# One row tile of the adjacency loaded in 32 by 32 blocks and turned by VectorE

## The chip, the core and the metric

The kernel runs on one core of one Trainium2 chip. The metric is the device time of one launch in microseconds (us), the median of three runs. Within the program the times below count from the first instruction of the profiled execution.

## What is computed

Four graph layers in a row, each followed by a layer norm, on 1354 nodes with 256 features and one dense 1354 by 1354 float32 adjacency matrix `adj`. Only the first layer is touched here:

```python
# layer 1: binarised features and weight, aggregated over the adjacency
bw = sign(weight)
ba = maximum(sign(x), 0)
xw = ba @ bw.T
x  = layernorm(x + relu(adj @ xw))
# layers 2 to 4 then use adj as well: adj @ x, masked attention, mean over neighbours, softmax(...) * adj
```

## The kernel before

The nodes are cut into eleven tiles of 128 (the last has 74). Everything after the first layer reads the adjacency transposed, as `adjT` (128 partitions, 11 column tiles, 1408 wide), so the first layer builds `adjT` while it aggregates. Here is the work for row tile i:

- SyncE's queue (SP) loads the tile into one of three slots of `adj_rows` (L312). From the fourth tile on it first waits until the tile that used the slot has been turned.
- TensorE (PE) turns the tile with eleven transposes of 128 by 128 into three PSUM banks (`adj_turn`, L1302).
- ScalarE (ACT) copies each bank twice (`adj_evac`): into `adjT` (L494) and, rounded, into `hi` (L495).
- VectorE (DVE) computes `lo`, the rest `adjT - hi`, for the first two bank groups (`lower_bits`, L755). GpSimd (POOL) does it for the third (L375).
- TensorE aggregates: `agg_a(i)`, L1375, is 22 matmuls, for each of eleven k one with `hi` and one with `lo`. Before k = 0 it waits for the first `lo` group, before k = 4 for the second, before k = 8 for POOL's.
- VectorE finishes the tile (`finish_a`: L798, the statistics L782 to L785, whose last writes `veps`), POOL takes the reciprocal square root (`rstd`, L386), VectorE writes `nmr` (`shift_a`, L806), and ScalarE applies both (L527).

The order on each engine is written by hand. TensorE does `agg_a(i)` and then `adj_turn(i + 2)`, and before `agg_a(4)` a short `spread_dots` (L1358). VectorE's step i is: finish tile i, a few dot products (L814, from step 4 on; three of them in step 4), first `lo` group of tile i+2, `nmr` of tile i, second `lo` group of tile i+2. POOL's step i is `rstd` of tile i and then its `lo` group of tile i+2. ScalarE's is `adj_evac(i)` and then the norm of tile i-2. Every engine takes its instructions in order. When the eleventh `agg_a` is through, TensorE goes on with the second layer (`z_part`, L1394), which needs the normed features one tile at a time.

Of the kernel before, what the change touches and what calls it, by code (L numbers as in the profile page):

```python
# [9 lines left out]
ACT = mybir.ActivationFunctionType  # L10
AX = mybir.AxisListType

P = 128
# [29 lines left out]
def gnn_stack(nc, x, adj, w0, w_sa, a_sa, w_gcn, b_gcn, wa, ba, wb, bb, w2, b2, w3, out):  # L43
    N, D = x.shape
    T = -(-N // P)
    FULL = N // P
    TAIL = N - FULL * P
    NP = T * P
# [5 lines left out]
    BANKS_T = -(-T // EB)  # L54
# [16 lines left out]
    BLOCK = 32  # L71
    QUADS = P // BLOCK
    SUMB = [2, 5, 2]
    BLOCKED = NC + 1
    NB3 = [2, 3, 5]
    FIN4 = {1: 0, 5: 1, 8: 2}
# [8 lines left out]
    def grp(g):  # L85

        return g * EB, min(g * EB + EB, T)

    ctx = ExitStack()
    with ctx:  # L90
# [5 lines left out]
        def sem(name):  # L96
            return Count(ctx.enter_context(nc.semaphore(name)))
# [71 lines left out]
        def at(name, offset, shape, dt=F32):  # L169
            return nc.alloc_sbuf_tensor_at(name, shape, dt, offset=base + offset)  # L170

        adj_rows = at("adj_rows", 0, [P, 3, NP])
        hi = at("hi", 3 * LONG, [P, PARTS, T, P], F32R)
        lo = at("lo", 6 * LONG, [P, PARTS, T, P], F32R)
        xw = at("xw", 9 * LONG, [P, T, D], F32R)
# [42 lines left out]

        adj_in = [sem("adj_in_0"), sem("adj_in_1"), sem("adj_in_2")]
        adj_in_tail = sem("adj_in_tail")  # L220
        rows2_in = [sem("rows2_in_even"), sem("rows2_in_odd")]
        x_in = [sem(f"x_in_{n}") for n in range(PAIRS)]
        w0_in, w_in, wsa_in, a_in, col_in = sem("w0_in"), sem("w_in"), sem("wsa_in"), sem("a_in"), sem("col_in")
# [74 lines left out]
        def tiles(g):  # L298

            c0, c1, _ = chunk(g)  # L300
            return range(c0 // P, -(-c1 // P))

        def across(columns, n, r):

            return columns[0:r, n:n + 1].to_broadcast([r, P])

        @block.sync
        def _(sp):
            def load_rows(i):
                if i >= 3:  # L310
                    sp.wait_ge(adjT_turned.sem, (i - 2) * BANKS_T)
                sp.dma_start(adj_rows[:, i % 3, 0:N], adj[i * P:(i + 1) * P, :]).then_inc(adj_in[i % 3].sem, 16)  # L312

            sp.dma_start(w0n[:, :, :], w0.rearrange("(k p) d -> p k d", p=P)).then_inc(w0_in.sem, 16)
# [3 lines left out]
            sp.wait_ge(pads_zero.sem, 1)  # L318
            sp.dma_start(x_all[0:64, FULL, :], x[FULL * P:FULL * P + 64, :]).then_inc(x_in[PAIRS - 1].sem, 16)
            sp.dma_start(x_all[64:TAIL, FULL, :], x[FULL * P + 64:N, :]).then_inc(x_in[PAIRS - 1].sem, 16)  # L320
            for i in range(FULL):
                load_rows(i)
            sp.wait_ge(adjT_turned.sem, (FULL - 2) * BANKS_T)
            b = FULL % 3
            sp.dma_start(adj_rows[0:64, b, 0:N], adj[FULL * P:FULL * P + 64, :]).then_inc(adj_in_tail.sem, 16)
            sp.dma_start(adj_rows[64:TAIL, b, 0:N], adj[FULL * P + 64:N, :]).then_inc(adj_in_tail.sem, 16)
# [150 lines left out]
        def _(act):  # L477
# [8 lines left out]
            def adj_evac(i, groups=range(BANKS_T)):  # L486
                r = kk(i)
                if i >= PARTS:
                    act.wait_ge(agga_done.sem, i - PARTS + 1)
                for g in groups:  # L490
                    k0, k1 = grp(g)
                    act.wait_ge(adjT_turned.sem, i * BANKS_T + g + 1)
                    src = bank((i % 2) * BANKS_T + g, 0, (k1 - k0) * P).rearrange("p (k n) -> p k n", n=P)[:, :, 0:r]
                    nc.scalar.activation(adjT[:, k0:k1, i * P:i * P + r], src, ACT.Copy)  # L494
                    nc.scalar.activation(hi[:, i % PARTS, k0:k1, 0:r], src, ACT.Copy).then_inc(adjT_banks_read.sem, 1)  # L495
# [242 lines left out]
        def _(dve):  # L738
            own = Own(dve, dve_own.sem)

            nc.vector.memset(dots[:, 0, 0:P], 0.0).then_inc(zeros_ready.sem, 1)
            own.link(nc.vector.memset(x_all[:, FULL, :], 0.0))
            nc.vector.memset(adj_rows[:, :, N:NP], 0.0).then_inc(pads_zero.sem, 1)
            nc.vector.memset(rdeg[:, :], 0.0)
            nc.vector.memset(dent[:, :], 1.0)
# [4 lines left out]
            def lower_bits(i, groups=range(BANKS_T)):  # L750
                r = kk(i)
                for g in groups:
                    k0, k1 = grp(g)
                    dve.wait_ge(adjT_banks_read.sem, BANKS_T * i + g + 1)
                    last = nc.vector.tensor_tensor(lo[:, i % PARTS, k0:k1, 0:r], adjT[:, k0:k1, i * P:i * P + r],  # L755
                                                   hi[:, i % PARTS, k0:k1, 0:r], ALU.subtract)
                    last.then_inc(lo_ready.sem, 1)

            def positive(n):
                t0, t1 = 2 * n, min(2 * n + 2, T)  # L760
# [71 lines left out]
            for i in range(T):  # L832
                if i == 2:
                    dot_columns()
                finish_a(i)
                if i == 4:
                    dve.wait_ge(ubc_ready.sem, 1)
                    left_dot(0)
                    left_dot(1)
                if i >= 4:  # L840
                    left_dot(i - 2)
                if i + 2 < T:
                    lower_bits(i + 2, range(0, 1))
                shift_a(i)
                if i + 2 < T:
                    lower_bits(i + 2, range(1, LOW))
            left_dot(T - 2)
# [422 lines left out]
        def _(pe):  # L1270
# [12 lines left out]
            def adj_turn(i):  # L1283
                r = kk(i)
                if i == FULL:
                    pe.wait_ge(adj_in_tail.sem, 32)
                else:
                    pe.wait_ge(adj_in[i % 3].sem, 16 * (i // 3 + 1))
                for g in range(BANKS_T):
                    k0, k1 = grp(g)  # L1290
                    if i == 0:
# [87 lines left out]
            for i in range(T):  # L1379
                if i == 4:  # L1380
                    spread_dots()
                agg_a(i)
                if i + 2 < T:
                    adj_turn(i + 2)


# [420 lines left out]
```

## Time and profile before

| | us |
|---|---|
| median of three runs | 473.91 (473.73 to 473.94) |
| the profiled execution, its own time | 474.03 |
| its span, first to last instruction | 472.2 |
| first layer: first `agg_a` to the last | 13.2 to 53.3 |

The span is the part of the profiled execution that the trace covers; 1.8 us lie around it. Each row of a time line gives the start, the duration, the engine, the source line, the operation, output and input with their shapes, and in brackets the idle time before it with what ended it. Successive starts on one engine can be closer than the durations, since an engine overlaps the end of one instruction with the next.

### The profile page before, as it was taken

The page shows a single profiled execution, that of the slowest core. Times are in us where ns is not written, and L with a number is a line of the kernel's source. Part 1 is how long each engine was busy: PE and PEld are TensorE (multiplying, and loading weights), DVE is VectorE, ACT ScalarE, POOL GpSimd, SP SyncE. Part 2 cuts the span into 40 slices and gives each one's busy share as a digit, 9 for nine tenths or more (in the row PEclk, how much of TensorE's full clock was granted, in tenths as well). Part 3 has the DMA queues.
Part 4 walks back from the last instruction along what each step waited for, and adds up shares of the span by engine and source line. Part 5 has one row for each costly group of instructions (what it writes and reads, how often), then busy time and mean ns, then how long its engine had stood idle before and what let it go on. Part 6 is the DMA issues. An engine that isn't in the chain of part 4 may idle for free.

```text
span 472.2 us, 5614 instructions
## 1 busy us (share of the span) xinstructions
PE 461.6 (98%) x1838; PEld 302.9 (64%) x1838; DVE 373.1 (79%) x830; ACT 231.3 (49%) x408; POOL 189.2 (40%) x186
## 2 busy tenths in 40 slices
PE   8999999999999999999999999999999999999993
PEld 7999755545555588787544444554557546778882
DVE  4688799999998689858137746999955697899984
ACT  6979529991888543333434532442333475342200
POOL 1444665631425036954001541452440073456641
PEclk9999999999999999999999999999999999999999
DMA  8856310001359100000000000000000000000001
GB/s 304 279 177 184 128 36 0 1 1 59 117 185 202 32 0 1 0 1 1 0 1 0 0 1 1 1 0 0 1 1 1 0 1 1 0 20 16 22 24 40
DMA packets 16500, 21.73 MB, mean 46 GB/s; under 512 B 9328, under 2 KB 13060, under 8 KB 16472
## 3 DMA queue, kind: packets, MB, share of 16 engines
q1 hardware_dynamic: 14648, 19.28, 13.2%
q10 hardware_dynamic: 1360, 1.31, 0.8%
q0 software_dynamic: 464, 0.79, 0.7%
q8 instruction: 15, 0.25, 0.2%
q14 instruction: 13, 0.11, 0.1%
HBM read 19.99 MB, written 1.39 MB: 45 GB/s over the span
## 4 chain that ended last, share of the span: by engine, by line
PE 75%; DVE 18%; issue 4%; DMA 1%; POOL 1%; ACT 0%; SPq 0%; POOLq 0%; DVEq 0%
PE psum L1590 16%; PE psum L1433 11%; PE psum L1394 11%; PE psum L1690 8%; PE psum L1375 6%; PE psum L1627 6%; PE psum L1570 3%; DVE ST L1082 3%; PE psum L1302 3%; PE psum L1542 2%; PE psum L1456 2%; PE psum L1661 2%; DVE rm L1031 2%; PE psum L1484 2%; DVE stats L782 1%
## 5 line engine op out<-in xcount | busy, mean ns | idle before, releaser
L1590 PE MATMUL psum<-QT,xT 128*128 128x512 f32 (+3 forms) x264 | 108.0, 542 | 0.0
L459 POOL TENSOR_TENSOR es<-es,ST 128x512 f32<-128x512 f32 (+3 forms) x60 | 75.9, 1265 | 55.2 <-ACT ST L658 53.5
L653 ACT ACTIVATE ST<-psum 128x512 f32<-128x512 f32 (+3 forms) x66 | 36.1, 546 | 91.6 <-DVE rm L1031 81.8
L1590 PEld LDWEIGHTS psum<-QT,xT 128*128 128x128 f32 (+1 forms) x264 | 48.2, 186 | 42.5 <-issue 35.9
L1031 DVE TENSOR_TENSOR rm<-psum,rm 128x512 f32<-128x512 f32 (+3 forms) x60 | 37.4, 623 | 40.6 <-PE psum L1590 40.4
L1690 PE MATMUL psum<-Wh,ST 128*128 128x256 f32 (+3 forms) x242 | 55.1, 380 | 0.0
L1627 PE MATMUL psum<-ST,Wh 128*128 128x512 f32 (+3 forms) x132 | 54.4, 543 | 0.6 <-DVE ST L1082 0.6
L386 POOL TENSOR_TENSOR rstd<-veps,nhalf 128x1 f32<-128x1 f32 (+1 forms) x44 | 29.2, 664 | 64.0 <-DVE veps L785 64.0
L414 POOL TENSOR_TENSOR esumb<-esumb,eb 128x1354 f32<-128x1354 f32 (+1 forms) x10 | 34.5, 3450 | 46.3 <-ACT eb L560 46.3
L1433 PE MATMUL psum<-eb,x_all 128*128 128x512 f32 (+3 forms) x132 | 51.9, 542 | 0.0
L1394 PE MATMUL psum<-adjT,x_all 128*128 128x512 f32 (+3 forms) x132 | 50.1, 542 | 0.0
L658 ACT ACTIVATE ST<-ST 128x512 f32<-128x512 f32 (+3 forms) x66 | 37.8, 578 | 25.0 <-DVE ST L1078 22.4
L1690 PEld LDWEIGHTS psum<-Wh,ST 128*128 128x128 f32 (+3 forms) x242 | 44.5, 186 | 8.2
L1082 DVE TENSOR_TENSOR ST<-ST,adjT 128x512 f32<-128x512 f32 (+3 forms) x66 | 46.8, 709 | 1.5 <-POOL es L459 1.5
L1627 PEld LDWEIGHTS psum<-ST,Wh 128*128 128x128 f32 (+1 forms) x132 | 24.9, 190 | 25.5 <-issue 19.2
L1394 PEld LDWEIGHTS psum<-adjT,x_all 128*128 128x128 f32 (+1 forms) x132 | 25.0, 190 | 24.7 <-issue 21.1
L1078 DVE TENSOR_TENSOR ST<-ST,psum 128x512 f32<-128x512 f32 (+3 forms) x66 | 40.0, 614 | 0.1
L1433 PEld LDWEIGHTS psum<-eb,x_all 128*128 128x128 f32 (+1 forms) x132 | 24.8, 190 | 22.6 <-issue 19.6
L456 POOL COPY es<-ST 128x512 f32<-128x512 f32 (+1 forms) x6 | 3.4, 559 | 82.7 <-ACT ST L658 82.7
L1484 PE MATMUL psum<-maskT,xhl 128*128 128x512 f32 (+1 forms) x132 | 30.3, 380 | 0.2
L1375 PE MATMUL psum<-xw,hi 128*128 128x256 f32 (+3 forms) x121 | 30.3, 290 | 0.0
L545 ACT ACTIVATE signs<-signs 128x1354 bf16<-128x1354 bf16 (+1 forms) x22 | 29.3, 1332 | 0.7
(176 smaller groups left out, 775.0 us busy)
## 6 DMA issues: line engine op xcount, KB each, us to landing
adj_rows<-in_adj_dram SPq DMA_DIRECT2D x10, 677.0 KB, 5.5
rows<-in_adj_dram SPq DMA_DIRECT2D x10, 677.0 KB, 4.0
out_dram<-xs SPq DMA_DIRECT2D x10, 128.0 KB, 1.7
W<-in_L_gnn_W_stack_dram SPq DMA_DIRECT2D x2, 512.0 KB, 5.3
W3B<-in_L_gnn_W_stack_dram SPq DMA_DIRECT2D x8, 128.0 KB, 3.7
x_all<-in_x_dram ACTq DMA_DIRECT2D x3, 256.0 KB, 4.8
x_all<-in_x_dram SPq DMA_DIRECT2D x2, 256.0 KB, 5.2
adj_rows<-in_adj_dram SPq DMA_DIRECT2D x1, 338.5 KB
```

The lines of the kernel that those rows point to most:

```text
L459: nc.gpsimd.tensor_tensor(es[0:r, g % 2, 0:w], es[0:r, g % 2, 0:w], buf(g)[0:r, j, 0:w], ALU.add)\
L658: nc.scalar.activation(buf(g)[0:r, j, 0:w], buf(g)[0:r, j, 0:w], ACT.Exp).then_inc(prob_ready.sem, 1)
L1031: nc.vector.tensor_tensor(m, src, m, ALU.max).then_inc(rm_step.sem, 1)
L1078: nc.vector.tensor_tensor(buf(g)[0:r, j, 0:w], buf(g)[0:r, j, 0:w], psum[0:r, 7, 0:w], ALU.add).then_inc(sub_done.sem, 1)
L1082: nc.vector.tensor_tensor(buf(g)[0:r, j - 2, 0:w], buf(g)[0:r, j - 2, 0:w], adjT[0:r, j - 2, c0:c1], ALU.mult)\
L1375: last = nc.tensor.matmul(psum[0:r, 6 + i % 2, 0:D], part[0:kk(k), i % PARTS, k, 0:r], xw[0:kk(k), k, :], start=(k == 0 and part is hi), s ...
L1394: last = nc.tensor.matmul(bank(c * KD + m, 0, c1 - c0), x_all[0:r, j, m * P:(m + 1) * P], adjT[0:r, j, c0:c1], start=(j == 0), stop=(j == ...
L1433: last = nc.tensor.matmul(bank(c * KD + m, 0, c1 - c0), x_all[0:r, j, m * P:(m + 1) * P], ebs[j % RING][0:r, c0:c1], start=(j == 0), stop= ...
L1484: last = nc.tensor.matmul(bank(c * KD + m, 0, c1 - c0), xhl[0:r, j, part, m * P:(m + 1) * P], maskT[j % MASKS][0:r, c0:c1], start=(j == 0 ...
L1590: last = nc.tensor.matmul(psum[0:r, SB[n % 3], 0:w], xT[l][:, k, j * P:j * P + r], QT[:, k, c0:c1], start=(k == 0), stop=(k == KD - 1))
L1627: last = nc.tensor.matmul(bank(SUMB[g] + m, 0, w), Wh[0][0:r, j, m * P:(m + 1) * P], buf(g)[0:r, j, 0:w], start=(j == 0), stop=(j == T - 1))
L1690: last = nc.tensor.matmul(psum[0:r, NB3[i % 3], 0:D], buf(g)[0:q, j, n * P:n * P + r], Wh[1][0:q, j, :], start=(j == 0), stop=(j == T - 1))
```

## The change

Row tile 6 no longer passes TensorE and PSUM. SP loads it as 16 column-and-row blocks (and three for the last, narrow column tile), 19 DMAs in all, each with runs of 32 floats (128 bytes), so that the 32 by 32 blocks already lie in the partition quadrant in which they are needed. VectorE's transpose turns each 32 by 32 block within its quadrant, and one instruction over 1408 columns writes tile 6 of `adjT`. It stands in VectorE's step 2. ScalarE then makes only the `hi` copies of tile 6, from `adjT`. The waits that counted turned tiles leave tile 6 out. The buffer `adj_blocks` lies apart from `adj_rows`, so loads 7 to 9 use the slots as before.

```diff
+    BLOCKS = [6]
...
+        def turned(i):
+            return BANKS_T * (i - sum(1 for b in BLOCKS if b < i))
...
 def load_rows(i):
     if i >= 3:
-        sp.wait_ge(adjT_turned.sem, (i - 2) * BANKS_T)
+        sp.wait_ge(adjT_turned.sem, turned(i - 2))
...
+            def load_row_blocks(n, a0, a1):
+                i = BLOCKS[n]
+                rows = adj[i * P:(i + 1) * P, :]
+                whole = rows[:, 0:FULL * P].rearrange("(b u) (t a v) -> a b u t v", u=BLOCK, a=QUADS, v=BLOCK)
+                for a in range(a0, a1):
+                    for b in range(QUADS):
+                        sp.dma_start(adj_blocks[a * BLOCK:(a + 1) * BLOCK, n, 0:FULL * P].rearrange("u (t c) -> u t c", c=P)[:, :, b * BLOCK:(b + 1) * BLOCK],
+                                     whole[a, b]).then_inc(block_in[n].sem, 16)
...
             for i in range(FULL):
-                load_rows(i)
+                if i not in BLOCKS:
+                    load_rows(i)
+                if i == 2:
+                    load_row_blocks(0, 0, 1)
+                if i == 4:
+                    load_row_blocks(0, 1, 3)
+                if i == 5:
+                    load_row_blocks(0, 3, 4)
...
 def adj_evac(i, groups=range(BANKS_T)):
+                if i in BLOCKS:
+                    act.wait_ge(block_turned.sem, BLOCKS.index(i) + 1)
+                    for g in groups:
+                        k0, k1 = grp(g)
+                        nc.scalar.activation(hi[:, i % PARTS, k0:k1, 0:r], adjT[:, k0:k1, i * P:i * P + r], ACT.Copy)\
+                            .then_inc(adjT_banks_read.sem, 1)
+                    return
...
+            def turn_blocks(n):
+                i = BLOCKS[n]
+                dve.wait_ge(block_in[n].sem, 16 * (QUADS * QUADS - (-TAIL // BLOCK)))
+                nc.vector.transpose(adjT[:, :, i * P:(i + 1) * P], adj_blocks[:, n, :].rearrange("p (t c) -> p t c", c=P)).then_inc(block_turned.sem, 1)
...
                 shift_a(i)
+                if i + 4 in BLOCKS:
+                    turn_blocks(BLOCKS.index(i + 4))
                 if i + 2 < T:
                     lower_bits(i + 2, range(1, LOW))
...
                 agg_a(i)
-                if i + 2 < T:
+                if i + 2 < T and i + 2 not in BLOCKS:
                     adj_turn(i + 2)
```

What stands in a row on VectorE in its step 2, around `nmr` of tile 2 (`lo` here is that of tile 4; the changed kernel's rows have its own line numbers). Before:

```order
L785 TENSOR_SCALAR veps<-mv 128x1
L755 TENSOR_TENSOR lo<-adjT,hi 128x512
L806 SCALAR_TENSOR_TENSOR nmr<-mv,rstd 128x1
L755 TENSOR_TENSOR lo<-adjT,hi 128x512
L798 SCALAR_TENSOR_TENSOR vbuf<-psum,x_all 128x256
```

And in the changed kernel:

```order
L826 TENSOR_SCALAR veps<-mv 128x1
L791 TENSOR_TENSOR lo<-adjT,hi 128x512
L847 SCALAR_TENSOR_TENSOR nmr<-mv,rstd 128x1
L798 STREAM_TRANSPOSE adjT<-adj_blocks 128x11x128
L791 TENSOR_TENSOR lo<-adjT,hi 128x512
L839 SCALAR_TENSOR_TENSOR vbuf<-psum,x_all 128x256
```

The transpose has come between `nmr` of tile 2 and the second `lo` group of tile 4.

SyncE's queue at the same stage, from the first row tile to the tail. Before:

```order
L312 DMA adj_rows<-in_adj_dram 128x1354 x3
L312 DMA adj_rows<-in_adj_dram 128x1354 [waits adjT_turned] x7
L325 DMA adj_rows<-in_adj_dram 64x1354 [waits adjT_turned]
L326 DMA adj_rows<-in_adj_dram 10x1354
L327 DMA W<-in_L_gnn_W_dram 128x2x256
```

And in the changed kernel:

```order
L320 DMA adj_rows<-in_adj_dram 128x1354 x3
L335 DMA adj_blocks<-in_adj_dram 32x10x32 x4
L339 DMA adj_blocks<-in_adj_dram 32x4x32
L320 DMA adj_rows<-in_adj_dram 128x1354 [waits adjT_turned] x2
L335 DMA adj_blocks<-in_adj_dram 32x10x32 x8
L339 DMA adj_blocks<-in_adj_dram 32x4x32
L339 DMA adj_blocks<-in_adj_dram 32x4x10
L320 DMA adj_rows<-in_adj_dram 128x1354 [waits adjT_turned]
L335 DMA adj_blocks<-in_adj_dram 32x10x32 x4
L320 DMA adj_rows<-in_adj_dram 128x1354 [waits adjT_turned] x3
```

Five block DMAs stand behind the third row tile, ten between tile 4 and tile 5, and four between tile 5 and tile 7.

## Rows read from the trace of the kernel before

**Rows 1.** The page: busy time, share of the span and instructions of each engine.

```profile
PE 461.6 (98%) x1838; PEld 302.9 (64%) x1838; DVE 373.1 (79%) x830; ACT 231.3 (49%) x408; POOL 189.2 (40%) x186
```

**Rows 2.** Chain that ended last, in order (start, us, what), first layer.

```profile
29.38 2.63 PE psum L1375 x22
32.02 1.20 PE psum L1302 x11
...
48.05 5.27 PE psum L1375 x44
```

**Rows 3.** Time line of TensorE: `agg_a(4)`, `adj_turn(6)`, `agg_a(5)`, start of `agg_a(6)`.

```profile
29.14 0.37 PE L1375 MATMUL psum<-xw,hi 128*128 128x256 f32 x1
...
30.17 0.28 PE L1375 MATMUL psum<-xw,hi 128*128 128x256 f32 x1
...
31.85 1.37 PE L1302 MATMUL psum<-ident,adj_rows 128*128 128x128 f32 x11
32.97 0.37 PE L1375 MATMUL psum<-xw,hi 128*128 128x256 f32 x1
...
36.80 0.36 PE L1375 MATMUL psum<-xw,hi 128*128 128x256 f32 x1
```

**Rows 4.** Time line of VectorE, steps 2 to 4.

```profile
27.08 0.15 DVE L785 TENSOR_SCALAR veps<-mv 128x1 f32<-128x1 f32 x1
...
28.28 0.94 DVE L806 SCALAR_TENSOR_TENSOR nmr<-mv,rstd 128x1 f32<-128x1 f32 x1 [0.44 <-POOL rstd L386]
29.14 0.68 DVE L755 TENSOR_TENSOR lo<-adjT,hi 128x512 fp32r<-128x512 f32 x1
29.75 0.41 DVE L798 SCALAR_TENSOR_TENSOR vbuf<-psum,x_all 128x256 f32<-128x256 f32 x1
...
30.87 0.15 DVE L785 TENSOR_SCALAR veps<-mv 128x1 f32<-128x1 f32 x1
31.35 0.69 DVE L755 TENSOR_TENSOR lo<-adjT,hi 128x512 fp32r<-128x512 f32 x1 [0.32 <-ACT hi L495]
...
32.93 0.42 DVE L798 SCALAR_TENSOR_TENSOR vbuf<-psum,x_all 128x256 f32<-128x256 f32 x1
...
35.23 0.69 DVE L755 TENSOR_TENSOR lo<-adjT,hi 128x512 fp32r<-128x512 f32 x1
```

**Rows 5.** Time line of GpSimd, steps 2 and 4.

```profile
27.32 0.93 POOL L386 TENSOR_TENSOR rstd<-veps,nhalf 128x1 f32<-128x1 f32 x1 [2.70 <-DVE veps L785]
28.22 0.99 POOL L375 TENSOR_TENSOR lo<-adjT,hi 128x384 fp32r<-128x384 f32 x1
...
34.30 0.72 POOL L386 TENSOR_TENSOR rstd<-veps,nhalf 128x1 f32<-128x1 f32 x1 [0.16 <-DVE veps L785]
36.32 1.14 POOL L375 TENSOR_TENSOR lo<-adjT,hi 128x384 fp32r<-128x384 f32 x1 [1.30 <-ACT hi L495]
```

**Rows 6.** Time lines of GpSimd and VectorE: a `lo` of POOL, a dot product beside it.

```profile
23.53 1.08 POOL L375 TENSOR_TENSOR lo<-adjT,hi 128x384 fp32r<-128x384 f32 x1 [1.48 <-ACT hi L495]
...
23.79 1.10 DVE L823 CUSTOM_DVE_ANT_0 dots<-Wsa,a_b 128x256 f32<-128x256 f32 x1
```

**Rows 7.** Time line of VectorE: its transpose before the second layer, and what follows.

```profile
58.34 1.65 DVE L856 STREAM_TRANSPOSE nslb<-lefts 128x1408 f32<-128x1408 f32 x1
59.91 0.49 DVE L814 CUSTOM_DVE_ANT_0 dots<-x_all,ubc 128x256 f32<-128x256 f32 x1
```

**Rows 8.** Time line of ScalarE: a strided and a dense copy of tile 5.

```profile
32.15 0.52 ACT L494 ACTIVATE adjT<-psum 128x384 f32<-128x384 f32 x1
32.52 0.53 ACT L495 ACTIVATE hi<-psum 128x384 fp32r<-128x384 f32 x1
```

**Rows 9.** Line L335, eight DMAs of 128 KB in runs of 128 bytes.

```profile
L335 SPq DMA_DIRECT2D W3B<-in_L_gnn_W_stack_dram x8: 585/675/1831, 142.1 to 150.7; - x8
...
DMA to landing us min/median/max: 3.0/3.7/4.6
```

**Rows 10.** Windows: busy time by engine, granted clock, DMA share, GB/s.

```profile
24.00:27.00 3.00, 3.00 (x29) 3.00 (x28) 2.82 (x11) 2.55 (x6) 0.61 (x1) 1.00 0.52 165
```

More of the change, by code:

```diff
@@ L172, in gnn_stack @@
         adj_rows = at("adj_rows", 0, [P, 3, NP])
+        adj_blocks = at("adj_blocks", 15 * LONG, [P, len(BLOCKS), NP])
         hi = at("hi", 3 * LONG, [P, PARTS, T, P], F32R)
@@ L220, in gnn_stack @@
         adj_in_tail = sem("adj_in_tail")
+        block_in = [sem(f"block_in_{n}") for n in range(len(BLOCKS))]
+        block_turned = sem("block_turned")
         rows2_in = [sem("rows2_in_even"), sem("rows2_in_odd")]
@@ L320, in _ @@
             sp.dma_start(x_all[64:TAIL, FULL, :], x[FULL * P + 64:N, :]).then_inc(x_in[PAIRS - 1].sem, 16)
-            for i in range(FULL):
-                load_rows(i)
-            sp.wait_ge(adjT_turned.sem, (FULL - 2) * BANKS_T)
+            def load_row_blocks(n, a0, a1):
[6 more added lines that the diff above has]
+                                     whole[a, b]).then_inc(block_in[n].sem, 16)
+                for a in range(a0, min(a1, -(-TAIL // BLOCK))):
+                    c0, c1 = FULL * P + a * BLOCK, min(FULL * P + (a + 1) * BLOCK, N)
+                    sp.dma_start(adj_blocks[a * BLOCK:(a + 1) * BLOCK, n, FULL * P:NP].rearrange("u (b v) -> u b v", v=BLOCK)[:, :, 0:c1 - c0],
+                                 rows[:, c0:c1].rearrange("(b u) v -> u b v", u=BLOCK)).then_inc(block_in[n].sem, 16)
+            for i in range(FULL):
+                if i not in BLOCKS:
[6 more added lines that the diff above has]
+                    load_row_blocks(0, 3, 4)
+            sp.wait_ge(adjT_turned.sem, turned(FULL - 2))
             b = FULL % 3
@@ L489, in adj_evac @@
                     act.wait_ge(agga_done.sem, i - PARTS + 1)
+                if i in BLOCKS:
[5 more added lines that the diff above has]
+                    return
                 for g in groups:
                     k0, k1 = grp(g)
-                    act.wait_ge(adjT_turned.sem, i * BANKS_T + g + 1)
+                    act.wait_ge(adjT_turned.sem, turned(i) + g + 1)
                     src = bank((i % 2) * BANKS_T + g, 0, (k1 - k0) * P).rearrange("p (k n) -> p k n", n=P)[:, :, 0:r]
@@ L742, in _ @@
             own.link(nc.vector.memset(x_all[:, FULL, :], 0.0))
+            own.link(nc.vector.memset(adj_blocks[:, :, FULL * P:NP], 0.0))
             nc.vector.memset(adj_rows[:, :, N:NP], 0.0).then_inc(pads_zero.sem, 1)
@@ L1287, in adj_turn @@
                 else:
-                    pe.wait_ge(adj_in[i % 3].sem, 16 * (i // 3 + 1))
+                    pe.wait_ge(adj_in[i % 3].sem, 16 * (i // 3 + 1 - sum(1 for b in BLOCKS if b < i and b % 3 == i % 3)))
                 for g in range(BANKS_T):
```

## The prediction

> **What bounds the kernel now.** I read the page first: TensorE is busy 98% of the span [rows 1]. Then the chain that ended last, in order of time. Through the whole first layer it is TensorE alone: aggregate (22 matmuls, 2.63 us), turn (11 transposes, 1.20 us), aggregate, with nothing between them [rows 2]. TensorE's time line says the same, one step from `agg_a(5)` to `agg_a(6)` takes 36.80 - 32.97 = 3.83 us [rows 3]. So time taken off TensorE here is time off the kernel, as long as no operand comes late. The question is how near the operands are to being late. For that I read VectorE's time line beside TensorE's. VectorE's second `lo` group of tile 4 starts at 29.14 and with its 0.69 us is there at 29.83 [rows 4]. The ninth matmul of `agg_a(4)`, which needs it, starts at 30.17 [rows 3]. The slack is 0.34 us, and it is the smallest in this layer, because in step 2 VectorE also has the four dot products of L823 [rows 6]. The change puts an instruction of over 1.5 us just ahead of that group.
>
> **What is removed.** Eleven transposes of tile 6 on TensorE, on the chain: 1.20 us [rows 2]. The last two aggregates, with no turn between them, take 5.27 us together, 2.63 each [rows 2], so nothing hidden returns when the turn goes. 3.83 - 2.63 gives the same 1.20. ScalarE loses three of its copies and no one waits for them. Ideal sum: 474.03 - 1.20 = 472.8.
>
> **What is added on VectorE.** One transpose over 1408 columns. VectorE has just such an instruction later: start 58.34, next start 59.91, so it holds the engine 1.57 us [rows 7]. Here it writes runs of 128 columns into `adjT` in place of one dense row. No row shows that for VectorE. ScalarE's copy of the same shape into `adjT` takes 0.52 against 0.53 us for the dense one [rows 8], so I take 1.57, and for the bounds 1.2 and 2.2. TensorE's wait below moves one for one with it.
>
> For the cost of turning alone a rule of the Trainium skill can be held against these rows. VectorE: DVE Perf Modes, the three transpose paths and the rules for authors, gives 390 ns for one 128 by 128 bf16 turn on TensorE and 311 ns on VectorE, and advises TensorE for a full 128 by 128 tile. An estimate from that page, eleven times 311 ns, would be 3.4 us in place of 1.57 and would add 1.9 us to the sum below. The duration in this trace decides, and the sum does without it.
>
> Now step by step. Only what is late on TensorE counts.
>
> *Step 2.* The second `lo` group of tile 4 starts at 29.14 + 1.57 = 30.71 and ends at 31.40. TensorE stands before its ninth matmul from 30.17 to about 31.43: a wait of 1.26 us. `agg_a(4)` ends 1.26 us late. Now the turn of tile 6 is missing, so `agg_a(5)` could start at 31.85 + 1.26 = 33.11, against 32.97 before [rows 3]. The gain is already gone.
>
> *Step 3.* VectorE's `veps` of tile 3 moves from 30.87 to 32.44. The first `lo` group of tile 5 follows at once, 32.52 to 33.21 (ScalarE's part, for which it waited 0.32 us before, is long there) [rows 4]. `agg_a(5)` starts at 33.24. Then `nmr`: in step 2 of the trace `rstd` and POOL's own `lo` follow each other at 27.32 and 28.22, and `nmr`, an operation on one column that takes 0.15 us elsewhere, takes 0.94 and ends with POOL's `lo` [rows 4, 5]. A dot product takes 1.10 us with POOL's `lo` running from 23.53 to 24.61 [rows 6], a like one 0.49 with POOL at rest [rows 7]. So POOL's tensor operation shuts out VectorE's with two SBUF inputs. In step 3 before, POOL's `lo` came late and there was no meeting. In the changed kernel step 3 stands as step 2 does, since the copies of tile 5 are ready (the last starts at 32.52 [rows 8]) before `rstd` is. From `veps` to the second `lo` group step 2 took 29.14 - 27.08 = 2.06 us [rows 4]: 32.44 + 2.06 = 34.50, done 35.19. The ninth matmul of `agg_a(5)` is due 1.03 us after its first (30.17 - 29.14), at 34.27, and waits 0.95. `agg_a(6)` could now start at 36.80 + 0.27 + 0.95 = 38.02, late by 1.22 us.
>
> *Step 4.* The finish of tile 4 starts 0.61 us behind that `lo` group, at 35.11, before 32.93. The first `lo` group of tile 6 came 35.23 - 32.93 = 2.30 us later, behind three dot products [rows 4], so 37.41. POOL's `rstd` ends 35.02 - 32.93 = 2.09 us after the finish began [rows 4, 5], at 37.20, and POOL's `lo` of tile 6 comes straight behind it, as its inputs are there: `nmr` of tile 3 is done by 34.6, and ScalarE's norm and three `hi` copies, some 0.5 us each [rows 8], are through by 36.7. Before, that POOL operation came at 36.32, when both of VectorE's groups were out [rows 5]. Now it holds from 37.2 to 38.2 or 38.3, the first `lo` group waits to about 38.15 and is done at 38.85, and `agg_a(6)` starts at 38.88: another 0.86 us. Late by 2.08 us in all. The next `lo` groups follow without a gap, and VectorE's steps (about 3.0 us) are again shorter than TensorE's 3.83, so nothing more is added.
>
> Whether the `lo` group of L755 is shut out like L806 and L823 the trace doesn't show. It has the same kind of operands, two SBUF inputs. The Trainium skill, SBUF — State Buffer, the section on the two separate sides, says that a VectorE operation with two SBUF inputs and a GpSimd operation exclude each other for the whole instruction. By that rule the third wait comes, and without it the sum is 1.33 us (1.22 and 0.11 for the plain order).
>
> **What is added on the DMA side.** Nineteen DMAs for one. The eight of L335, three times as many runs each, take SP 0.59 to 0.68 us apiece as a rule and 1.83 at worst, and land in 3.0 to 4.6 us [rows 9]. Their pace, 128 KB in about 0.7 us, is that of the issue. The 677 KB of tile 6 are then 3.7 us of transfer against some 2 us in whole rows. Five are issued by 8 us, behind the first three tiles, which also wait to be turned. Ten follow load 4 (issued at 13.2) until about 19.5 and push load 5 from 17.5 to about that. Four follow it until 22. DMA was about full until 24 us and at 0.52 from 24 to 27 [rows 10], so the backlog of 2 to 4 us falls into that gap. I expect tile 5 by about 26.5 (its turn starts near 27.6) and the last block by 27.5 to 28.5, before VectorE asks at 29.2. Cost zero. The cover is 1 to 2 us thin, and each us beyond it costs a us, since the second `lo` group stands behind the transpose. Load 7 waits for tile 4 as before, and loads 8 and 9 come no later. Behind the first layer everything starts from its last aggregate, so the delay goes through to the end: the second layer is TensorE's again.
>
> **Sum.** 474.03 - 1.12 + 1.26 + (0.13 + 0.95) + 0.86 = 476.1 for the profiled execution, with the turn counted from start to start, 32.97 - 31.85 = 1.12 (with the chain's 1.20 it would be 0.08 less). That one lies 0.12 above the median of the runs, so 476.0.
>
> **The rivals.**
> 1. Faster, 472.8: the slack takes the transpose in and the 1.20 us stay. Against it: the slack is 0.34 us and the transpose 1.57. It needs VectorE some 1.3 us earlier in step 2 than the trace has it. 7%.
> 2. Only the first wait, with the meetings with POOL missing or short: step 3 then gives 33.24 + 0.50 - 0.27 of lateness, about +0.5 us in all, 474.5; with small waits up to 0.9, 474.8. For it: the meetings hang on 0.1 us of timing. Against it: step 2 of the trace is the very same order and had its meeting. 13%.
> 3. The meeting in step 3 but not in step 4: 1.33 us, 475.3. 17%.
> 4. The blocks late: if the last lands at 31 instead of before 29.2, 1.8 us more than the forecast, 477.9. It decides from 29.2 on. For it: DMA at its limit up to 24 us and some 5,400 runs of 128 bytes in place of 128 rows. Against it: rows 9. 14%.
>
> **How the numbers follow.** The forecast itself, 475.6 to 476.8 with the bounds of the transpose, has 49%. A difference of 0.2% (0.95 us) is about what a measurement of this kernel can tell from none. Slower by more: forecast and rivals 3 and 4, 80%. Within: 13%. Faster: 7%. The range leaves out rival 1 and the far end of rival 4: 474.4 to 478.0.
>
> **What would show it.** TensorE's time line: a hole of about 1.3 us inside `agg_a(4)` before its ninth matmul, one of 0.9 inside `agg_a(5)`, one of under 1 before `agg_a(6)`, then none. VectorE: the transpose 1.57 to 1.65 us long at about 29.2 with no idle time before it, `nmr` of tile 3 some 0.9 us long, the first `lo` group of tile 6 longer than 0.69. If the transpose has idle time before it that ends with a DMA, rival 4 holds. If `nmr` takes 0.15, rival 2. If there is no hole in `agg_a(4)`, the main step is wrong.

## The result: slower, by the mechanism forecast, and one us further

The changed kernel takes 477.03 us (median of five, 475.94 to 479.41) against 473.91 before (473.45 to 473.97): ratio 1.0076, 95% interval 1.0063 to 1.0090. Slower was forecast at 476.0 with a range of 474.4 to 478.0. The prediction's sum gave 476.1 for the profiled execution. That execution took 479.41 us, the longest of the five, so the profile shows the change at its worst, 3.3 us beyond the sum. The spread is the first thing to see: 0.7% between the runs of the changed kernel, 0.1% before.

The page, busy time, share of the span and instructions of each engine (answers to [rows 1]). TensorE's busy time is the same although eleven transposes have gone (1838 to 1827); its share has fallen by a point. TensorE's ends are modelled, so some of its waiting is counted as busy: the waits in brackets in its time line below add up to 4.70 us, by start times the waits are 5.79. I go by start times.

```profile
PE 462.0 (97%) x1827; PEld 302.4 (63%) x1827; DVE 376.3 (79%) x832; ACT 230.1 (48%) x405; POOL 189.6 (40%) x186
```

The chain that ended last, in order of time, in the first layer (answers to [rows 2], which were TensorE alone). Columns: start, us, what.

```profile
24.64 0.45 PE psum L1345 x4
25.09 0.20 SPq L320
25.29 0.04 issue
25.34 0.43 SPq L335
...
26.81 5.49 DMA adj_blocks<-in_adj_dram
32.30 0.02 issue
32.33 1.65 DVE adjT L798
33.97 0.57 DVE lo L791
...
36.82 0.85 issue
37.67 0.68 DVE lo L791
...
40.65 1.41 DVE lo L791
42.06 0.14 issue
42.19 2.88 PE psum L1418 x22
45.07 1.20 PE psum L1345 x11
...
58.73 49.98 PE psum L1437 x132
```

From 25 us on the chain runs over SyncE's queue, the last block DMA, the transpose and then VectorE's `lo` groups; TensorE takes it over again with `agg_a(6)` at 42.19. The chain's step onto the queue at 25.09 falls inside the issue of load 5, which had begun at 24.86, so it doesn't say what held the queue; the issues do, below. Behind the layer nothing has changed: from the start of the second layer to the end of the span it is 477.6 - 58.73 = 418.9 us, and 472.2 - 53.32 = 418.9 before.

TensorE's time line, the rows with a wait and the first matmuls of `agg_a(4)` and `agg_a(5)` (answers to [rows 3]):

```profile
29.67 1.42 PE L1345 MATMUL psum<-ident,adj_rows 128*128 128x128 f32 x11 [1.21 <-DMA adj_rows<-in_adj_dram]
...
31.28 0.36 PE L1418 MATMUL psum<-xw,hi 128*128 128x256 f32 x1
...
34.60 0.39 PE L1418 MATMUL psum<-xw,hi 128*128 128x256 f32 x1 [2.11 <-DVE lo L791]
...
36.49 0.36 PE L1418 MATMUL psum<-xw,hi 128*128 128x256 f32 x1
...
38.41 0.39 PE L1418 MATMUL psum<-xw,hi 128*128 128x256 f32 x1 [0.73 <-DVE lo L791]
...
42.19 0.36 PE L1418 MATMUL psum<-xw,hi 128*128 128x256 f32 x1 [0.65 <-DVE lo L791]
```

The three holes stand where the prediction put them: the ninth matmul of `agg_a(4)`, the ninth of `agg_a(5)`, the first of `agg_a(6)`. One more is ahead of them, before the turn of tile 5. VectorE's time line (answers to [rows 4]):

```profile
28.99 0.95 DVE L847 SCALAR_TENSOR_TENSOR nmr<-mv,rstd 128x1 f32<-128x1 f32 x1 [0.44 <-POOL rstd L414]
32.33 1.65 DVE L798 STREAM_TRANSPOSE adjT<-adj_blocks 128x1408 f32<-128x1408 f32 x1 [2.39 <-DMA adj_blocks<-in_adj_dram]
33.89 0.65 DVE L791 TENSOR_TENSOR lo<-adjT,hi 128x512 fp32r<-128x512 f32 x1
...
36.78 0.97 DVE L847 SCALAR_TENSOR_TENSOR nmr<-mv,rstd 128x1 f32<-128x1 f32 x1 [0.44 <-POOL rstd L414]
37.67 0.68 DVE L791 TENSOR_TENSOR lo<-adjT,hi 128x512 fp32r<-128x512 f32 x1
...
40.57 1.48 DVE L791 TENSOR_TENSOR lo<-adjT,hi 128x512 fp32r<-128x512 f32 x1
```

and GpSimd's (POOL) beside it (answers to [rows 5]):

```profile
36.72 1.01 POOL L403 TENSOR_TENSOR lo<-adjT,hi 128x384 fp32r<-128x384 f32 x1
...
40.33 1.17 POOL L403 TENSOR_TENSOR lo<-adjT,hi 128x384 fp32r<-128x384 f32 x1
```

The transpose takes 1.65 us and the next start is 1.56 us behind it, as in [rows 7]. Ahead of it VectorE waits 2.39 us for the last block. `nmr` of tile 3 takes 0.97 us and the first `lo` group of tile 6 takes 1.48 in place of 0.69: the two meetings with POOL. Both end as if their own work began when POOL's did end: POOL's `lo` is over at 37.73 and `nmr` at 37.75, and 41.50 plus 0.69 is near the 42.05 at which the `lo` group ends. That also answers what the trace of before left open, whether an L755 can be shut out: it can. The rule of the Trainium skill on the shared port pair (SBUF — State Buffer, two separate sides) agrees with these rows.

Why the block was late stands on SyncE's queue, line L335 of the changed kernel, the sixteen large block DMAs (answer to [rows 9]): durations of the issue, min, median and max in ns, and the time to landing.

```profile
L335 SPq DMA_DIRECT2D adj_blocks<-in_adj_dram x16: 432/466/3227, 4.8 to 26.8; - x16
...
DMA to landing us min/median/max: 3.8/6.8/8.6
```

The maximum has to be placed in time before it explains anything. The same line in the window from 6.5 to 7.5 us, and the queue's time line from the first of the ten blocks ahead of load 5:

```profile
L335 SPq DMA_DIRECT2D adj_blocks<-in_adj_dram x1: 3227/3227/3227, 6.3 to 6.3; - x1
```

```profile
14.28 9.56 SPq L335 DMA_DIRECT2D adj_blocks<-in_adj_dram  x8
```

The issue of 3.23 us belongs to the first five blocks. It delays nothing, since load 3 behind them has to wait for its slot until 12.7 us. What counts is the row of eight: at the usual 0.47 us they would take 4 us with the gaps, and they take 9.56. Four of them were held, from 16.42, 19.40, 20.49 and 21.60 us, for 2.94, 1.04, 1.07 and 2.24 us. So load 5, behind them, went out at 24.9 and not at 17.5, and the last block at 26.8.

Since the starts of the executions differ by up to 1 us, I compare below the length of the first layer in each profiled execution, from the first matmul of `agg_a(0)` to the first of the second layer. Before it is 53.32 - 13.17 = 40.15 us, in the changed kernel 58.73 - 13.89 = 44.84. Of the 5.4 us by which the profiled executions differ, 4.69 lie in this layer and 0.72 ahead of it.

### The profile page after: what moved, and what is told of

The parts are those of the page before. It is cut to its first block, busy times and chain, and to the rows that moved or that the text cites. A ratio compares the mean times of both kernels' runs of the same rounds, so it can differ in the third digit from the quotient of the medians.

```text
span 477.6 us, 5608 instructions
## 1 busy us (share of the span) xinstructions
PE 462.0 (97%) x1827; PEld 302.4 (63%) x1827; DVE 376.3 (79%) x832; ACT 230.1 (48%) x405; POOL 189.6 (40%) x186
## 3 DMA queue, kind: packets, MB, share of 16 engines
HBM read 19.99 MB, written 1.39 MB: 45 GB/s over the span
## 4 chain that ended last, share of the span: by engine, by line
PE 71%; DVE 20%; issue 4%; DMA 3%; POOL 1%; ACT 0%; SPq 0%; ACTq 0%; POOLq 0%; DVEq 0%
PE psum L1633 16%; PE psum L1476 10%; PE psum L1437 10%; PE psum L1733 8%; PE psum L1670 6%; PE psum L1418 5%; PE psum L1613 3%; DVE ST L1125 3%; PE psum L1585 2%; PE psum L1499 2%; PE psum L1704 2%; DVE rm L1074 2%; PE psum L1345 2%; PE psum L1527 2%; DVE stats L823 2%
## 5 line engine op out<-in xcount | busy, mean ns | idle before, releaser
L1670 PEld LDWEIGHTS psum<-ST,Wh 128*128 128x128 f32 (+1 forms) x132 | 24.9, 190 | 25.5 <-issue 19.1
```

Source lines behind the costliest of these rows:

```text
L1670: last = nc.tensor.matmul(bank(SUMB[g] + m, 0, w), Wh[0][0:r, j, m * P:(m + 1) * P], buf(g)[0:r, j, 0:w], start=(j == 0), stop=(j == T - 1))
```

## The experiments

The two theories behind the first four runs: the loss is VectorE's (the transpose in front of `lo`, and POOL), with the transfers on top; or it is the transfers alone.

### The changed kernel again

> The changed kernel once more, beside the others. In its first trace three things came together: the VectorE part of the forecast (holes of 2.3, 0.9 and 1.0 us before the ninth matmul of agg_a(4), the ninth of agg_a(5) and the first of agg_a(6)), tile 5 late (TensorE waited 1.2 us for it) and the last block late (the transpose waited 2.4 us). If the late transfers are a matter of the moment, the time here spreads again over 476 to 479 us; if they are fixed, it stays within 0.3% of itself.

477.05 us (475.95 to 478.18, six runs), ratio 1.0071 (1.0057 to 1.0086). The loss repeats and so does the spread. In this trace the layer takes 56.09 - 12.92 = 43.17 us, 1.7 less than in the first, and the transpose waits less:

```profile
29.72 1.65 DVE L798 STREAM_TRANSPOSE adjT<-adj_blocks 128x1408 f32<-128x1408 f32 x1 [0.75 <-DMA adj_blocks<-in_adj_dram]
```

So what varies is when the blocks land, 2.39 us too late in one execution and 0.75 in the other. Tile 5 is in time here, and was 1.42 us late in the first trace. That lateness cost nothing of its own: the second `lo` group waits for the transpose, whether `agg_a(4)` has begun early or late.

This trace has one thing more that the first has not: from 34 to 36 us the granted clock is 0.50 (TensorE's lower level, 1.2 GHz), after the hole in `agg_a(4)`; the matmuls there start 0.21 us apart in place of 0.12. The hole in the first trace was no shorter (2.29 us, here 2.07), with no such fall. In the layer it can't be seen: VectorE was what `agg_a(6)` waited for.

### Tile 6 by one ordinary DMA

```diff
+                else:
+                    sp.wait_ge(adjT_turned.sem, turned(i - 2))
+                    sp.dma_start(adj_blocks[:, 0, 0:N], adj[i * P:(i + 1) * P, :]).then_inc(block_in[0].sem, 16)
-                if i == 2:
-                    load_row_blocks(0, 0, 1)
-                if i == 4:
-                    load_row_blocks(0, 1, 3)
-                if i == 5:
-                    load_row_blocks(0, 3, 4)
...
-                dve.wait_ge(block_in[n].sem, 16 * (QUADS * QUADS - (-TAIL // BLOCK)))
+                dve.wait_ge(block_in[n].sem, 16)
```

> Tile 6 comes by one ordinary DMA of whole rows into adj_blocks, issued where load 6 stood before; the rest is the changed kernel, transpose included (the data of tile 6 is not in block order, so its part of the result is another). Theory (VectorE is 2.1 us of the loss, the block transfers the rest): 476.0 us, steady, transpose with no idle time before it. Rival (the whole loss is the transfers): 472.8 us.

475.34 us (475.17 to 476.04) against 473.73, ratio 1.0036 (1.0023 to 1.0049). The layer takes 55.33 - 12.97 = 42.36 us, 2.21 more than before; the sum of the prediction was 2.08. The median of the time is 1.6 us above before and not 2.1: the profiled execution, 476.04, is the longest of its five, so the traces settle the mechanism here and the size is 1.6 to 2.2. Here the transfers are out of it, and TensorE's time line reads almost like the prediction:

```profile
28.94 0.37 PE L1415 MATMUL psum<-xw,hi 128*128 128x256 f32 x1
31.20 0.39 PE L1415 MATMUL psum<-xw,hi 128*128 128x256 f32 x1 [1.07 <-DVE lo L788]
33.10 0.36 PE L1415 MATMUL psum<-xw,hi 128*128 128x256 f32 x1
35.02 0.39 PE L1415 MATMUL psum<-xw,hi 128*128 128x256 f32 x1 [0.74 <-DVE lo L788]
...
38.81 0.36 PE L1415 MATMUL psum<-xw,hi 128*128 128x256 f32 x1 [0.64 <-DVE lo L788]
```

The prediction had 31.43, 33.24 and 38.88 for the second, third and last of these starts, from a first at 29.14. By start times, each hole against the due time: 31.20 - (28.94 + 1.03) = 1.23, 35.02 - (33.10 + 1.03) = 0.89, and `agg_a(6)` 5.71 us behind `agg_a(5)` in place of 3.83, of which 0.89 is the hole before, so 0.99. VectorE alone makes the kernel slower; that the loss was all transfers is out.

### The blocks, turned by TensorE

```diff
-            return BANKS_T * (i - sum(1 for b in BLOCKS if b < i))
+            return BANKS_T * i
...
-                if i in BLOCKS:
+                if False:
                     act.wait_ge(block_turned.sem, BLOCKS.index(i) + 1)
...
-                if i + 4 in BLOCKS:
-                    turn_blocks(BLOCKS.index(i + 4))
...
+                elif i in BLOCKS:
+                    pe.wait_ge(block_in[0].sem, 16 * (QUADS * QUADS - (-TAIL // BLOCK)))
...
-                        last = nc.tensor.transpose(bank((i % 2) * BANKS_T + g, c, c + r), adj_rows[0:r, i % 3, k * P:(k + 1) * P],
+                        last = nc.tensor.transpose(bank((i % 2) * BANKS_T + g, c, c + r), (adj_blocks[0:r, 0, k * P:(k + 1) * P] if i in BLOCKS else adj_rows[0:r, i % 3, k * P:(k + 1) * P]),
...
-                if i + 2 < T and i + 2 not in BLOCKS:
+                if i + 2 < T:
```

> The nineteen block DMAs as in the changed kernel, but tile 6 is turned by TensorE from adj_blocks and copied by ScalarE as before; no transpose on VectorE (tile 6's part of the result is another). Theory (the transfers hold back SyncE's queue, load 5 and with it TensorE): 0.7 to 2.5 us slower than before, 474.6 to 476.4, unsteady, with TensorE waiting for adj_rows before the turn of tile 5. Rival (transfers harmless by themselves, only the wait of VectorE in front of lo costs): within 0.3 us of before.

474.19 us against 473.73, ratio 1.0011 (1.0002 to 1.0020): less than I expected, and more than nothing. The layer takes 40.73 us, 0.58 more than before, and TensorE does wait for tile 5:

```profile
27.90 0.77 PE L1345 MATMUL psum<-ident,adj_rows 128*128 128x128 f32 x5 [0.36 <-DMA adj_rows<-in_adj_dram]
```

The transfers by themselves cost about half a us. It is all tile 5's: `agg_a(4)` starts 0.57 us late and nothing after it waits, because the last block (issued at 25.0, landed by 30.1) is wanted only at 32.2. With VectorE asking at 29 they cost more: from 475.34 with one ordinary DMA to 477.05 with the blocks, run side by side, is 1.7 us. So the two halves don't add up (1.6 and 0.5 against 3.3).

The traces show what does add up: the 2.21 us of the run with one DMA, plus the wait of the transpose for its last block. In the changed kernel's two traces that is 2.21 + 2.39 = 4.60 and 2.21 + 0.75 = 2.96, and the layers are 4.69 and 3.02 us longer than before.

### Tile 9 in place of tile 6

```diff
-    BLOCKS = [6]
+    BLOCKS = [9]
...
-                if i == 2:
-                    load_row_blocks(0, 0, 1)
-                if i == 4:
-                    load_row_blocks(0, 1, 3)
-                if i == 5:
-                    load_row_blocks(0, 3, 4)
+                if 5 <= i <= 8:
+                    load_row_blocks(0, i - 5, i - 4)
...
-                if i + 4 in BLOCKS:
-                    turn_blocks(BLOCKS.index(i + 4))
                 if i + 2 < T:
                     lower_bits(i + 2, range(1, LOW))
+                if i + 3 in BLOCKS:
+                    turn_blocks(BLOCKS.index(i + 3))
```

> The same change made to tile 9 instead of tile 6: four portions of block DMAs behind loads 5 to 8, transpose in VectorE's step 6 behind the second lo group of tile 8. There VectorE has idle time and the lo groups are over 2 us ahead of TensorE. Theory (the loss of the change is its place): the 1.2 us of the turn stay, less 0.1, 472.8 us. Rival (any transpose on VectorE in this layer costs more than the turn, or the block DMAs hold loads 7 to 10 up): 474 us or more.

473.24 us against 473.73, ratio 0.9990 (0.9981 to 0.9998): the same change, three tiles on, no longer loses. But it gains 0.5 us where 0.9 was expected. VectorE's time line, steps 6 and 7:

```profile
42.52 1.64 DVE L794 STREAM_TRANSPOSE adjT<-adj_blocks 128x1408 f32<-128x1408 f32 x1
...
46.26 0.96 DVE L843 SCALAR_TENSOR_TENSOR nmr<-mv,rstd 128x1 f32<-128x1 f32 x1
47.15 0.68 DVE L787 TENSOR_TENSOR lo<-adjT,hi 128x512 fp32r<-128x512 f32 x1
```

`nmr` of tile 7 meets POOL's `lo` of tile 9 and takes 0.96 us, so the `lo` groups of tiles 9 and 10 come just too late. In this execution the layer takes 52.78 - 12.78 = 40.00 us, 0.15 less than before; of the turn's 1.12 us, waits from the start of `agg_a(9)` on have taken the rest. The 0.5 us of the medians is more than the layer shows, and no trace accounts for the difference.

### POOL's operation out of the way

```diff
+                if i in (5, 6):
+                    r = 1
                 nc.gpsimd.tensor_tensor(lo[:, i % PARTS, k0:k1, 0:r], adjT[:, k0:k1, i * P:i * P + r], hi[:, i % PARTS, k0:k1, 0:r],
```

> The run with one ordinary DMA for tile 6, and POOL's lo groups of tiles 5 and 6 cut to one column per block (their other columns are left out, so the result is another). Theory (two of the three holes come from POOL's tensor operation that shuts VectorE out): nmr of tile 3 falls from 0.97 to about 0.2 us, the first lo group of tile 6 from 1.49 to 0.69, and the time by 1.0 to 1.5 us, to 473.9 to 474.4. Rival (the holes are VectorE's own backlog): 475.3 as with full groups.

473.97 us against 473.41, ratio 1.0011 (1.0002 to 1.0020). The layer takes 53.57 - 12.84 = 40.73 us against 42.36 with full POOL groups: 1.6 us less. In the times, each against the kernel before run beside it, the loss falls from 1.6 to 0.6 us, as expected. The rows:

```profile
33.26 0.16 DVE L846 SCALAR_TENSOR_TENSOR nmr<-mv,rstd 128x1 f32<-128x1 f32 x1 [0.44 <-POOL rstd L413]
33.33 0.69 DVE L790 TENSOR_TENSOR lo<-adjT,hi 128x512 fp32r<-128x512 f32 x1
...
36.23 0.69 DVE L790 TENSOR_TENSOR lo<-adjT,hi 128x512 fp32r<-128x512 f32 x1
```

`nmr` is back to 0.16 and the first `lo` group of tile 6 to 0.69. Of TensorE's three holes only the first is left in the trace; by start times 0.08 us are left of the second and 0.20 of the third. So the two others were nearly all POOL's doing, and that VectorE was simply behind with its work is out. The control is the last run below.

### The transpose one place earlier

```diff
-                shift_a(i)
                 if i + 4 in BLOCKS:
                     turn_blocks(BLOCKS.index(i + 4))
+                shift_a(i)
```

> The run with one ordinary DMA for tile 6, with the transpose one place earlier, ahead of nmr of tile 2 instead of behind it. There VectorE idles 0.44 us for rstd and is then shut out by POOL's lo for some 0.8 us, 1.2 of the transpose's 1.57 us are to fit in. Theory: the hole in agg_a(4) shrinks from 1.2 to about 0.2 us and the time falls by 1.2 to 2.0 us, to 473.3 to 474.2. Rival (the place within the step doesn't matter, VectorE is short of time in all): 475.3.

473.60 us against 473.41, ratio 1.0002 (0.9993 to 1.0011): the loss of the one-DMA version gone within the noise, by one place in a row. The layer takes 53.45 - 13.04 = 40.41 us, 0.26 more than before.

```profile
27.61 1.64 DVE L795 STREAM_TRANSPOSE adjT<-adj_blocks 128x1408 f32<-128x1408 f32 x1
29.18 0.12 DVE L844 SCALAR_TENSOR_TENSOR nmr<-mv,rstd 128x1 f32<-128x1 f32 x1
29.21 0.69 DVE L788 TENSOR_TENSOR lo<-adjT,hi 128x512 fp32r<-128x512 f32 x1
...
35.30 1.49 DVE L788 TENSOR_TENSOR lo<-adjT,hi 128x512 fp32r<-128x512 f32 x1
```

and POOL's time line beside it:

```profile
28.08 1.00 POOL L400 TENSOR_TENSOR lo<-adjT,hi 128x384 fp32r<-128x384 f32 x1
```

The second `lo` group of tile 4 starts 29.21 - 13.04 = 16.17 us behind the layer's start, before the change 29.14 - 13.17 = 15.97. The 0.20 us stay within the slack of 0.34, and `agg_a(4)` has no hole: the transpose has filled the time in which VectorE waited for `rstd` and was shut out by POOL. Two things follow. POOL's `lo` ran from 28.08 to 29.08 while the transpose did, and neither became longer, so the transpose, with its one SBUF input, isn't shut out. And even here the turn's 1.20 us are not a gain: without the turn `agg_a(5)` asks sooner, and the trace has waits of 0.37 before it and 0.47 before `agg_a(6)`, whose `lo` group meets POOL again (1.49 us). By start times they are 0.55 and 0.84, more than the turn gave. This place can't be had with the blocks as they are, since they land after it, at 29.7 and 32.3 in the two traces.

### Long runs instead of short

```diff
-                        sp.dma_start(adj_blocks[a * BLOCK:(a + 1) * BLOCK, n, 0:FULL * P].rearrange("u (t c) -> u t c", c=P)[:, :, b * BLOCK:(b + 1) * BLOCK],
-                                     whole[a, b]).then_inc(block_in[n].sem, 16)
+                        sp.dma_start(adj_blocks[a * BLOCK:(a + 1) * BLOCK, n, b * 320:(b + 1) * 320],
+                                     rows[a * BLOCK:(a + 1) * BLOCK, b * 320:(b + 1) * 320]).then_inc(block_in[n].sem, 16)
```

> The changed kernel with the same nineteen DMAs at the same places, the sixteen large ones of the same 40 KB each, but each partition's share one run of 1280 bytes instead of ten of 128 (the data of tile 6 is not in block order, its part of the result is another). Theory (the many short runs fill SyncE's queue, so that an issue takes up to 3 us and load 5 and the last block come late): issues fall to under 0.5 us each, load 5 goes out near 18 to 20, the transpose has no idle time, 475.5 us. Rival (the number of DMAs holds the queue up): 477 us, issues of over 1 us.

475.78 us against 473.41, ratio 1.0047 (1.0034 to 1.0059), and steady again (475.45 to 476.17). The layer takes 55.63 - 13.27 = 42.36 us, to the hundredth what it took with one DMA. Load 5 went out at 20.2, the transpose has no idle time. The issues:

```profile
L335 SPq DMA_DIRECT2D adj_blocks<-in_adj_dram x16: 421/422/1234, 4.8 to 22.1; - x16
```

In this trace the same number of DMAs and the same bytes cost nothing when the runs are ten times as long. The medians leave that less sharp: 2.4 us above before here, 1.6 with one DMA, with intervals that overlap. Two issues were still held, for 1.23 and 1.12 us, not the under 0.5 I had expected of all. What the transfers cost in the changed kernel comes, in the traces, from the runs of 128 bytes. The windows (busy time of the engines, granted clock, DMA share, GB/s) show what the DMA engines did, first from 15 to 24 us in the changed kernel and then from 21 to 24 here:

```profile
15.00:18.00 3.00, 3.00 (x27) 2.87 (x26) 1.90 (x4) 3.00 (x8) 1.97 (x3) 1.00 1.00 336
18.00:21.00 3.00, 3.00 (x28) 3.00 (x27) 2.10 (x8) 2.75 (x7) 2.13 (x3) 1.00 1.10 304
21.00:24.00 3.00, 3.00 (x29) 3.00 (x27) 2.34 (x8) 2.66 (x6) 0.92 (x2) 1.00 0.52 82
```

```profile
21.00:24.00 3.00, 3.00 (x28) 3.00 (x27) 2.34 (x10) 3.00 (x7) 0.92 (x2) 1.00 0.94 292
```

Three of the four held issues of the changed kernel began with the DMA engines full (share 1.00 and 1.10); during the last one, 21.60 to 23.84 us, they were busy 0.45 of the time and moved 60 GB/s. So a full DMA goes with most of the holding, but doesn't explain it alone. The first five blocks say the same: from 6.3 us on DMA is as full in both kernels (1.05 and 374 GB/s, 1.06 and 369), and the fourth issue, begun at 6.3 and 6.2 us, takes 3.23 us with short runs and 0.42 with long ones. It is the short runs that are held; by what, no run here tells.

### Load 5 first

```diff
-                if i == 4:
-                    load_row_blocks(0, 1, 3)
                 if i == 5:
-                    load_row_blocks(0, 3, 4)
+                    load_row_blocks(0, 1, 4)
```

> The changed kernel with load 5 ahead of the ten blocks, so that all fourteen late blocks stand between load 5 and load 7. Theory: tile 5 is in time (TensorE doesn't wait for adj_rows), but the blocks go out from 17.5 us on instead of 13.5, and each us that the last one lands after 29 is a us: if they still go out by 27, the time is that of the changed kernel, 477 us, if the queue stays full, 478 to 480. Rival (load 5 was what mattered): 475.5.

476.12 us against 473.41, ratio 1.0053 (1.0039 to 1.0066); the interval overlaps that of the changed kernel (1.0057 to 1.0086), so a small gain is likely and not shown. The last block went out at 28.4 us. The profiled execution, the longest of its five at 477.09, has tile 5 in time and the transpose waiting 1.39 us for the last block. The layer takes 56.69 - 12.85 = 43.84 us, 3.69 more than before, and 2.21 + 1.39 is 3.60. (Here too the granted clock falls to 0.50 after the hole in `agg_a(4)`, from 33 to 35 us, and VectorE's chain covers it.) The theory's two parts hold, the lateness has moved from the one to the other; that the time would be no less than 477 was wrong. That load 5 was all that mattered is out as well, since a wait for the block is left.

### Tile 9, with the transpose in step 5 and `nmr` moved

```diff
                 if i + 2 < T:
                     lower_bits(i + 2, range(0, 1))
-                shift_a(i)
+                if i + 4 in BLOCKS:
+                    turn_blocks(BLOCKS.index(i + 4))
+                if i != 7:
+                    shift_a(i)
                 if i + 2 < T:
                     lower_bits(i + 2, range(1, LOW))
-                if i + 3 in BLOCKS:
-                    turn_blocks(BLOCKS.index(i + 3))
+                if i == 7:
+                    shift_a(i)
```

> The version with tile 9 in blocks, with two moves on VectorE: the transpose stands in step 5 ahead of nmr of tile 5, and in step 7 nmr comes behind the second lo group of tile 9, so that POOL's lo of tile 9 can't shut VectorE out between the two groups. In the trace with tile 9 in step 6 the first layer took 40.0 us from the first matmul of agg_a(0), against 40.15 before, since nmr of tile 7 took 0.96 us and the lo groups of tile 9 and 10 came late. Theory: the meeting costs 0.6 us, so the time falls below that version, 0.6 to 1.1 us under before (472.4 to 472.9 against 473.5). Rival (what was left of the gain there went elsewhere): as that version, 0.3 to 0.5 us under before.

473.03 us against 473.36, ratio 0.9991 (0.9982 to 1.0000). The layer takes 52.42 - 12.96 = 39.46 us, 0.69 less than before and 0.54 less than with tile 9 in step 6. That looks like the theory, and isn't: the meeting is still there. VectorE's two `lo` groups of tile 9, in one row of the time line, and POOL's `lo` beside them:

```profile
45.32 2.11 DVE L787 TENSOR_TENSOR lo<-adjT,hi 128x512 fp32r<-128x512 f32 x2
```

```profile
45.78 1.11 POOL L399 TENSOR_TENSOR lo<-adjT,hi 128x384 fp32r<-128x384 f32 x1
```

The first takes 0.69 us and the second, from 45.9 on, 1.51. POOL's `lo` of tile 9 runs from 45.78 to 46.89, so it now shuts out the `lo` group in place of `nmr`. The 0.54 us come from the other move. With the transpose out of step 6, step 7 stands earlier: its first `lo` group starts 32.36 us behind the layer's start in place of 32.88, 0.52 us sooner.

In the whole time the two versions can't be told apart: 0.9990 and 0.9991. The 0.33 us under before are what the rival gave (0.3 to 0.5), not the theory's 0.6 to 1.1. What a step without the meeting would be worth is not shown by this run. Neither version is more than 0.1% under the kernel before.

### Control: POOL's small groups without the change

The edit is that of the run with POOL's operation out of the way, made to the kernel before.

> The kernel before with POOL's lo groups of tiles 5 and 6 cut to one column per block (the other columns left out). Control for the run in which this was done with the transpose: in the kernel before POOL's work there meets no step of VectorE on TensorE's path. Theory: within 0.3 us of before. Rival (the shorter POOL operations gain something by themselves): 0.5 us or more faster.

473.60 us against 473.36, ratio 1.0003 (0.9994 to 1.0012). The layer takes 52.90 - 12.69 = 40.21 us, against 40.15: shortening POOL's groups gains nothing where they meet nothing.

## Why the prediction was right, and where it fell short

| step | forecast us | changed kernel, profiled | one DMA for tile 6 |
|---|---|---|---|
| hole before the ninth matmul of `agg_a(4)` | 1.26 | 2.29 | 1.23 |
| before `agg_a(5)` | 0.13 | 0.21 | 0.22 |
| hole before the ninth matmul of `agg_a(5)` | 0.95 | 0.89 | 0.89 |
| before `agg_a(6)` | 0.86 | 0.98 | 0.99 |
| turn of tile 6 gone, start to start | -1.12 | -1.12 | -1.12 |
| start of `agg_a(4)` | 0 | 1.42 | 0 |
| first layer against before | +2.08 | +4.69 | +2.21 |

The holes are start against due time: the first is 34.60 - (31.28 + 1.03), the other likewise. The rows before `agg_a(5)` and `agg_a(6)` are what is left of the distance between two starts: 36.49 - 31.28 = 5.21 us, less the 3.83 of before, less the hole of 2.29, plus the 1.12 of the turn, leaves 0.21. The start of `agg_a(4)` is 17.39 us behind that of `agg_a(0)` in place of 15.97. The terms add up to 4.67 and 2.21; the layers show 4.69 and 2.21. The 1.42 us of the row on `agg_a(4)` are tile 5's lateness, which only takes from the hole behind it: 2.29 + 1.42 = 3.71 is, but for 0.06, the forecast's 1.26 and the transpose's wait of 2.39.

**What held.** That the slack in front of the second `lo` group of tile 4 was 0.34 us and the transpose some 1.57, so that the turn's gain was gone at once. That the delay drags a second and a third wait behind it, since VectorE's step 3 then falls as its step 2 did, with POOL's `lo` between `rstd` and `nmr`. This was read from one row, 0.94 us for an operation of 0.15, and the run with the short POOL groups bears it out. (The dot product of 0.49 us in [rows 7] wasn't beside an idle POOL, which was issuing DMAs then; the trace of before has such dot products at 0.43 with POOL idle, right after the one of 1.10, and the reading stands.) That the third meeting would come, for which the trace of before had no row and which only the comparison of operand kinds supported. And that nothing behind the layer gives any of it back.

**What failed** is the step on the DMA side, "Cost zero". It measured 1.7 us between the medians with blocks and with one DMA, and 0.75 and 2.39 us of waiting in the two traces. It took the pace of the DMAs of L335, 0.59 to 0.68 us an issue, and had the last block out by 22 and landed by 28.5. The issues are no slower as a rule (0.47 us), but four of the eight large ones ahead of load 5 are held for 1 to 3 us: the last block went out at 24.5 and 26.8 in the two traces and landed at 29.7 and 32.3. From issue to landing it took 5.2 and 5.5 us, no more than the forecast had allowed behind its 22; the issue was what was late. I read the maximum of that row, 1.83 us, and passed it over as the worst of eight; it was the warning. I also counted the cover in GB/s, and the run with long runs moves the same bytes in time. The price of the lateness once it is there, one us for each us, was rival 4's, and it held in three traces (0.75, 1.39 and 2.39 us of waiting).

So the direction and the path on VectorE were right for the reason given, and the number was partly luck. The forecast of 476.0 had no lateness of the blocks in it; the run made for that case, with one DMA, had a median of 475.34. The measured 477.03 lies inside the range because the range reached 2.0 us beyond the forecast to take in part of rival 4, which had been given 14%. Of the eleven executions of the changed kernel two lie above its 478.0.

One line of the working can't be followed as written: rival 2's "33.24 + 0.50 - 0.27". From the prediction's own rows, with `nmr` at 0.15, it is -1.12 + 1.26 + 0.13 and 0.16 for the second wait, 0.43 in all, which is the +0.5 given.

The transpose itself was in the middle of its bounds, 1.56 us from start to start, so its strided output costs nothing beside the 1.57 of the dense one.

## What to carry to other kernels

Before a step is taken off the busiest engine, look up the smallest distance between an operand's arrival and its use there, and where in the helper engine's row the new work would stand; 1.2 us saved bought nothing here with 0.34 us of slack, and the same work one place earlier, in time that was already idle, cost nothing that the times show and gained nothing either. A small delay on one engine can bring operations of two others together that never met before: after shifting the rows of a step, look again for a row like `nmr`'s, six times as long as its work. Look at the neighbour's row too: moving `nmr` out of the way only put a `lo` group in its place. And a queue's pace is not the median of its issues when one issue in a row of eight took three times as long. But place the longest one in time first; here it was harmless, and four shorter ones were not.

## What was not expected of the hardware

DMAs of 32 by 10 runs of 128 bytes, issued in a row from SyncE's queue, were held for up to 3.23 us an issue; with runs of 1280 bytes the same bytes in the same number of DMAs were held for 1.23 us at most. Most of the holding came with the DMA engines full (share 1.00 to 1.10 from 15 to 21 us), but one hold of 2.24 us came while they were busy 0.45 of the time and moved 60 GB/s. VectorE's transpose (1.64 us) and a GpSimd tensor operation (1.00 us) ran side by side without either growing, while VectorE's operations with two SBUF inputs grew from 0.15 to 0.97 and from 0.69 to 1.49 us beside the same GpSimd operation.
